# Self-attention: softmax sums taken over two rounds at a time, and causal masks added behind two products

## What is computed

```python
q = (x @ Wq.T + bq).reshape(B, T, H, D)      # H = 16 heads of D = 32
k = (x @ Wk.T + bk).reshape(B, T, H, D)
v = (x @ Wv.T + bv).reshape(B, T, H, D)
scores = jnp.einsum('bqhd,bkhd->bhqk', q, k) * attn_scale[0]
scores = jnp.where(mask[None, None], -jnp.inf, scores)
attn = jax.nn.softmax(scores, axis=-1)
out = jnp.einsum('bhqk,bkhd->bqhd', attn, v).reshape(B, T, C)
return out @ Wo.T + bo
```

## Time and profile before

| | us |
|---|---|
| median of 3 runs | 3718.32 |
| lowest and highest | 3716.07, 3718.48 |
| the profiled execution | 3677.42 |
| its span, first to last instruction | 3675.7 |
| of it self-attention, about | 0 to 1825 |

### The profile page before, as it was taken

How to read it: one execution, slowest core, us unless ns; L and a number is a source line. 1 busy time by engine, 2 the same in 40 slices (tenths; PEclk the granted TensorE clock), 3 DMA queues, 4 the chain that set the end, 5 groups by cost and what they waited for, 6 DMA issues and landing times. The chain is left out here.

```text
span 3675.7 us, 65297 instructions
## 1 busy us (share of the span) xinstructions
PE 3247.4 (88%) x20385; PEld 2065.6 (56%) x20385; DVE 2202.0 (60%) x4409; ACT 1380.6 (38%) x3155; POOL 909.5 (25%) x889
## 2 busy tenths in 40 slices
PE   8998989899899998999797899999698892999991
PEld 4444444454444544444343677776577771888881
DVE  4645546455464544646354688887377773777775
ACT  2443434434343443434421466665000000444441
POOL 2000000000000000000032333333266665566661
PEclk8999999999999999999998999999899996999995
DMA  4122121221212222021075121211222212799996
GB/s 118 39 67 71 38 62 39 70 68 47 60 32 70 68 56 70 13 75 29 25 244 185 50 66 61 68 61 56 94 55 57 60 52 81 222 248 254 251 252 211
DMA packets 186637, 344.01 MB, mean 94 GB/s; under 512 B 36153, under 2 KB 53946, under 8 KB 185402
## 3 DMA queue, kind: packets, MB, share of 16 engines
q1 hardware_dynamic: 127674, 234.12, 22.5%
q0 software_dynamic: 31360, 56.82, 6.4%
q10 hardware_dynamic: 27392, 50.34, 3.7%
HBM read 206.96 MB, written 83.89 MB: 79 GB/s over the span
## 5 line engine op out<-in xcount | busy, mean ns | idle before, releaser
L549 DVE TENSOR_REDUCE sa_pmax<-sa_w 128x1 f32<-128x512 f32 (+3 forms) x1280 | 690.9, 603 | 398.9 <-PE sa_w L358 233.7
L491 ACT ACTIVATE sa_probs<-sa_s 128x512 f32<-128x512 f32 (+3 forms) x1280 | 614.0, 534 | 809.4 <-PE sa_s L393 416.7
L355 PE MATMUL sa_w<-sa_parts 96*128 96x512 f32 (+3 forms) x1280 | 488.2, 440 | 81.5 <-DVE sa_pmax L549 34.0
L393 PE MATMUL sa_s<-sa_parts 128*128 128x512 f32 (+3 forms) x1280 | 463.8, 416 | 23.5 <-ACT sa_probs L491 22.1
L296 POOL DMA_DIRECT2D scratch_attention_T<-sa_oT x32 | 17.6, 550 | 1782.7 <-DVE sa_oT L592 1519.7
L355 PEld LDWEIGHTS sa_w<-sa_parts 96*128 96x128 f32 x1280 | 236.1, 194 | 331.0 <-issue 178.7
L393 PEld LDWEIGHTS sa_s<-sa_parts 128*128 128x128 f32 x1280 | 241.0, 196 | 141.8 <-ACT sa_probs L491 90.7
L412 PE MATMUL sa_pv<-sa_probs,sa_values 128*32 128x512 f32 (+3 forms) x2560 | 299.8, 540 | 4.6 <-PE sa_w L338 2.4
L416 PE MATMUL sa_pv<-sa_probs,sa_ones 128*32 128x512 f32 (+3 forms) x2560 | 292.9, 528 | 0.0
L1318 POOL DMA_INDIRECT token_and_weight_of_slot<-rt_entry,rt_sl x256 | 256.3, 1001 | 143.1 <-issue 75.2
L1144 ACT ACTIVATE xa_sm<-xa_sm,xa_nmax 128x154 f32<-128x154 f32 x512 | 208.7, 409 | 64.5 <-DVE xa_nmax L1088 64.5
(11 more groups left out here) (242 smaller groups left out, 5704.8 us busy)
## 6 DMA issues: line engine op xcount, KB each, us to landing
ex_w<-in_w SPq DMA_DIRECT2D x138, 512.0 KB, 4.6
sa_parts<-sa_halves SPq DMA_DIRECT2D x384, 128.0 KB, 2.4
sa_xt<-in_xT SPq DMA_DIRECT2D x32, 1024.0 KB
scratch_attention_T<-sa_oT POOLq DMA_DIRECT2D x32, 256.0 KB, 2.5
on_at<-scratch_attention_T SPq DMA_DIRECT2D x32, 256.0 KB, 3.3
on_xr<-in_x SPq DMA_DIRECT2D x32, 256.0 KB, 3.5
scratch_x<-on_xn ACTq DMA_DIRECT2D x32, 256.0 KB, 2.2
scratch_x_T<-on_xnT ACTq DMA_DIRECT2D x32, 256.0 KB, 3.5
```

The source lines that it names most:

```text
L355: mm = nc.tensor.matmul(ps[:, 0:w], qparts[0:3 * HD, h, q0:q0 + P], kparts[0:3 * HD, h, k0:k0 + w], start=True, stop=s != 0)
L393: mm = nc.tensor.matmul(ps[:, 0:w], kparts[:, h, kb * P:(kb + 1) * P], qparts[:, h, q0:q0 + w], start=True, stop=not diag)
L491: nc.scalar.activation(probs[:, r % NPB, h, 0:w], sbank[n % NSB][:, 0:w], ACT.Exp).then_inc(exp_done, 1)
L549: dve.tensor_reduce(pmax[:, j * GH + h, s:s + 1], wbank[b][:, 0:width_], AX.X, ALU.max).then_inc(work_free[b], 1)
```

## The change

1. **Sums over pairs.** GpSimd adds the `probs` of rounds 2p and 2p + 1 into a new tile `both`, and TensorE multiplies `ones` by `both` once for a pair. `both` is one buffer: GpSimd waits for the sums' products of the pair before (`ones_done`) and for the exponentials; TensorE waits for `both_ready`. On the diagonal the first round of a pair is wider by 128 queries; these are copied first, then the rest is added. `probs` gets four buffers.
2. **`weighted` by pairs.** Both rounds' products with `values` and then the sums' products stand behind the next pair's second round. The loop is turned: a pair is peeled in front, and an iteration ends with the next group's pair 0, behind which the last pair's `weighted`, `take_raw`, `take_den` and the last `normalize` now stand.
3. **Masks.** The maxima's segments are ordered by key segment first and head second, and two that both need the mask are issued as product, product, mask, mask; so are the scores of heads 0 and 1. Groups of maxima in a round are cut at 4 and 6 in place of 3 and 5.
4. **Stores.** SyncE issues them in place of GpSimd: stores 0 and 1 behind `spread_parts(it + 1, 0)` and `(it + 1, 1)`, stores 2 and 3 at the end of its iteration, in front of `spread_parts(it + 1, 2)`. Two projections of chunk 3 move by one round.

```diff
     def segments(c):
-        return [(j, h, s) for j in range(QB) for h in range(GH) for s in range(c + 1)]
+        return [(j, h, s) for j in range(QB) for s in range(c + 1) for h in range(GH)]
...
-                 (3, 0): [("k", 0)], (3, 1): [("q", 0)], (3, 5): [("v", 0), ("k", 1)], (3, 6): [("q", 1)], (3, 9): [("v", 1)],
+                 (3, 0): [("k", 0)], (3, 1): [("q", 0)], (3, 5): [("k", 1)], (3, 6): [("v", 0), ("q", 1)], (3, 10): [("v", 1)],
...
-    NPB = 2
+    NPB = 4
...
+            def add_pair(it, p):
+
+                even, odd = 2 * p % NPB, (2 * p + 1) % NPB
+                c, k = round_at[2 * p]
+                wide, w = width(c, kbs(c)[k]), width(c, kbs(c)[k + 1])
+                pool.wait_ge(ones_done, it * NPAIR + (p + 1))
+                pool.wait_ge(exp_done, it * NU + (NSB + 2 * GH * (p + 1)))
+                apart(pool, passed)
+                if wide > w:
+                    pool.tensor_copy(both[:, :, w:wide], probs[:, even, :, w:wide]).then_inc(rest_copied, 1)
+                    pool.wait_ge(rest_copied, it * NREST + (rest_pairs.index(p) + 1))
+                    apart(pool, passed)
+                pool.tensor_tensor(both[:, :, 0:w], probs[:, even, :, 0:w], probs[:, odd, :, 0:w], ALU.add).then_inc(both_ready, 1)
...
+            def weighted(it, p):
+
+                for r in (2 * p, 2 * p + 1):
...
                     for h in range(GH):
                         a = HD * h
-                        nc.tensor.matmul(pvbank[0][a:a + HD, 0:w], values[:, kb, h, :], probs[:, r % NPB, h, 0:w],
-                                         start=first, stop=last)
-                    for h in range(GH):
-                        a = HD * h
-                        mm = nc.tensor.matmul(pvbank[1][a:a + HD, 0:w], ones[:], probs[:, r % NPB, h, 0:w],
-                                              start=first, stop=last)
+                        mm = nc.tensor.matmul(pvbank[0][a:a + HD, 0:w], values[:, kb, h, :], probs[:, r % NPB, h, 0:w],
+                                              start=kb == NKB - 1, stop=kb == QB * chunk_q(c))
                     mm.then_inc(pv_done, 1)
...
+                pe.wait_ge(both_ready, it * NPAIR + (2 + p + 1))
+                for h in range(GH):
+                    a = HD * h
+                    mm = nc.tensor.matmul(pvbank[1][a:a + HD, 0:w], ones[:], both[:, h, 0:w],
+                                          start=k == 1, stop=kb == QB * chunk_q(c))
+                mm.then_inc(ones_done, 1)
...
+                    maxima(it, i, segs[:4])
+                    score_masks([scores(it, r, 0), scores(it, r, 1)])
+                    maxima(it, i, segs[4:6])
+                    score_masks([scores(it, r, 2)])
+                    maxima(it, i, segs[6:])
+                    score_masks([scores(it, r, 3)])
```

More of the change, by code:

```diff
@@ L127, in free_at @@
         return it * uses[b] + (pre_uses[b] + WORK[key] // NWB + 1)
+    rest_pairs = [p for p in range(NR // 2) if rounds(round_at[2 * p][0]) - round_at[2 * p][1] <= QB]
+    NREST = len(rest_pairs)
     NSB = 3
-    NPB = 2
+    NPB = 4
+    NPAIR = NR // 2
     NDIST = 3 * GH * 16
@@ L188, in each_group, with each_from_second @@
             body(ITERS - 1, False)
+        def each_from_second(eng, pair):
+            with eng.Fori(0, ITERS - 1) as it:
+                for p in range(1, NPAIR):
+                    pair(it, p, True, (it, p - 1))
+                pair(it + 1, 0, True, (it, NPAIR - 1))
+            for p in range(1, NPAIR):
+                pair(ITERS - 1, p, False, (ITERS - 1, p - 1))
         @block.sync
@@ L372, in _ @@
             pe.wait_ge(consts_set, 1)
[L373 to L374 removed]
+            maxima(None, 0, [("m", 0, n) for n in range(len(segments(0)))])
             shift(None, 0, 0)
[L376 to L399 removed]
@@ new lines, in _, with scores @@
+            maxima(None, 0, [("m", 1, n) for n in range(EARLY)])
+            def scores(it, r, h):
+                c, k = round_at[r]
+                kb = kbs(c)[k]
+                n = GH * r + h
+                w = width(c, kb)
+                q0 = chunk_q(c) * CH
+                if k == 0:
+                    pe.wait_ge(shift_ready, it * (NC * GH) + (GH * c + h + 1))
+                pe.wait_ge(exp_done, it * NU + (n + 1 if n else NSB))
+                ps = sbank[n % NSB]
+                diag = kb < QB * (chunk_q(c) + 1)
+                mm = nc.tensor.matmul(ps[:, 0:w], kparts[:, h, kb * P:(kb + 1) * P], qparts[:, h, q0:q0 + w],
+                                      start=True, stop=not diag)
+                if not diag:
+                    mm.then_inc(s_ready, 1)
+                    return None
+                return ps[:, w - P:w]
@@ L400, in weighted, with score_masks @@
+            def score_masks(blocks):
+                for ps in blocks:
+                    if ps is not None:
+                        nc.tensor.matmul(ps, identb[:], maskT[:], start=False, stop=True).then_inc(s_ready, 1)
+            def weighted(it, p):
+                for r in (2 * p, 2 * p + 1):
                     c, k = round_at[r]
@@ L425, in body, with pair @@
+            def pair(it, p, more, behind):
+                for r in (2 * p, 2 * p + 1):
+                    c, k = round_at[r]
                     on_next = c == NC - 1
+                    i = it + 1 if on_next else it
                     segs = maxima_in(c, k) if more or not on_next else []
-                    maxima(segs[:3])
-                    scores(r, 0)
-                    scores(r, 1)
-                    maxima(segs[3:5])
-                    scores(r, 2)
-                    maxima(segs[5:])
@@ L441, in body @@
                             keys_queries(it, i, key[0], key[1])
-                    if r >= 1:
-                        weighted(r - 1)
-                weighted(NR - 1)
-            each_group(pe, body)
+                if behind is not None:
+                    weighted(*behind)
+            pair(0, 0, True, None)
+            each_from_second(pe, pair)
+            weighted(ITERS - 1, NPAIR - 1)
         @block.scalar
```

192 lines of the change are left out of this document (91 added, 101 removed).

## The result

The changed kernel takes 3772.41 us (median of four), the kernel before 3717.2 us: a ratio of 1.016, with a 95% interval of 1.015 to 1.018. One of the four executions was disturbed (4642 us): it is left out of the ratio but counted in that median, which would be 3769.68 us without it. The forecast was 3596 us, with a range of 3545 to 3655 us; the time lies 117 us above its end, and the sign is wrong. The profiled execution took 3766.8 us, its span 3764.9 us, 89 us more than the span of before.

The account below looks back on a forecast made before the run. TensorE was taken as the limit in places, VectorE's three banks nearly as close, ScalarE limiting rounds without maxima. Sums 114 + masks 12 - jump 3.5 = 122 us, off 3718.3 us, gave 3596 us; range 3545 to 3655 us.

Parts of the forecast that it names:

- What bounds the kernel: Self-attention: TensorE is the limit in places, ScalarE or VectorE's banks in others; TensorE is busy 94% of the loop.
- three kinds of rounds: Self-attention: rounds without maxima (3.47 us), rounds with maxima (4.64 us), and the jump back at a group's end.
- the part on the jump: Group's end: four maxima ahead of the scores lose 0.5 us at each of seven jumps, 3.5 us; bounds 0 and 10.
- chunk 2's pairs: Chunk 2's full pairs with maxima: 8.6 us against 9.28 us; 0.6 us gain taken for each of four.
- Masks, 12 us, bounds 0 and 48: 344 neighbouring pairs of masks on TensorE: each pair issued together saves 0.05 us, 0.7 of it counted; 12 us.
- The row that I read against a covered weight load: Earlier trace: a mask's weight load starts only at 240.03, so such loads aren't already covered and grouping gains.
- The sums, 114 us: All groups of self-attention: sums' products once for a pair save 14.7 us a group, 11.3 us in the last.
- a chunk's last pair: Narrow pairs of chunks 0 to 2: 0.3 us gain each, since `shift` waits for the last maxima anyway.
- GpSimd's adding costs nothing: Pairs' adds on GpSimd: 4.2 us each, needed by TensorE after 5.44 us at the tightest, so no cost.
- The slower rival: GpSimd's add slowed by other engines' memory use, TensorE waiting: no change at 8.3 us, 3768 us at 9; chance 0.08.
- The slow clock stays: Seven jumps: the same two idle times and the same 10 us of slow clock at each.
- Jump and SyncE's queue: Group's end: the jump loses 3.5 us; spreading chunk 2's parts behind store 3 costs nothing, with 2 us margin.

Follow-up runs that it names:

- the pairs alone: The changed kernel with the old order of segments, old cuts and each mask right behind its product: ratio 0.986 to the kernel before.
- the trace with the scores' masks: The changed kernel with old order, cuts and maxima's masks, keeping sums over pairs and the scores' masks two at a time: ratio 0.985 to the kernel before.
- the version with cuts at 2 and 4: Sums over pairs, scores' masks grouped, values' products each round, multiply on GpSimd, maxima cut at 2 and 4: 3543.7 us, ratio 0.964 to the kernel before.

## Why the prediction was wrong, point by point

- **What bounds the kernel**: held. Of the three kinds of rounds that I named, the rounds with maxima decide; I said there that VectorE's banks are as near to the limit as TensorE, and then didn't ask what the diff does to exactly those banks.
- **The failed step: the cuts.** The text knows them only as "four maxima now stand ahead of the scores", in the part on the jump, priced at 7 x 0.5 = 3.5 us with bounds of 0 and 10 us. They stand in every round with four maxima or more, not in seven jumps. Measured: 2.3% of the time on the kernel before, 2.5% in the changed kernel and 1.6% on the pairs alone, 60 to 93 us where I had 3.5 us. The prediction had all that was needed: "three products can be ahead of VectorE" stands in its own working of chunk 2's pairs, and the earlier trace rows has the 0.54 us and 0.59 us. 0.54 + 0.59 us less the 0.92 us of three products is a wait of 0.2 us at least, in each of the rounds, with two scores behind it. The pair length of 8.6 us was worked out with the old cuts; the pair of rounds 4 and 5 of chunk 2 measured 8.6 us with them and 9.6 us with the new ones. The larger part is in chunk 3, 77.7 us with the old cuts and 85.7 us with the new ones in the changed kernel.
- **Masks, 12 us, bounds 0 and 48**: wrong in sign under the new cuts, and the bounds didn't reach below nothing. With the old cuts neither grouping is told apart from nothing; with the new ones both together lose 1.1%, most likely since a grouped product is handed over later. Holding back a finished result was a cost that I didn't look for. The row that I read against a covered weight load is weak as well: the load at 240.03 lies inside the product recorded from 239.77 to 240.19.
- **The order of `segments`**: not priced. 0.2 to 0.3%, not clear of its interval.
- **The sums, 114 us**: the mechanism was right, the size was double. The pairs alone give 1.4%, 52 us of 3706. The term fails in places. Pairs without maxima take 6.29 us for a forecast of 6.41. Chunk 2's pairs at rounds 2, 4 and 8 take 9.5, 8.6 and 8.9 us, for 9.9, 9.4 and 9.9 us before and 8.6 us forecast. But a chunk's last pair, for which I said only that `shift` waits for the last maxima anyway, grew, and so did the pair with the scaling: TensorE waits for `mcol` and for VectorE behind GpSimd (rounds 6 and 7 of chunk 2, with the scaling: 12.2 us for 9.7 us). By the starts of the scores in the traces, chunk 1 takes 52.1 us a group for 50.6 before, where I had 3.0 us less (49.2 us in the trace with the scores' masks), and chunk 2 53.9 for 53.0, where I had 3.1 less; chunks 3 and 0 together are 9.1 us shorter, for 8.5 us forecast.
- **GpSimd's adding costs nothing**: its own time was right (4.57 us for 2048 columns, inside 3.61 to 5.10; 1.8 us of wait for it in all). The timeline of TensorE and GpSimd in the changed kernel's rounds without maxima answers to the earlier trace rows:

```profile
914.62 0.96 PE L428 MATMUL sa_s<-sa_parts 128*128 128x512 f32 x3
915.81 2.46 PE L428 MATMUL sa_s<-sa_parts 128*128 128x512 f32 x5 [0.22 <-ACT sa_probs L539]
918.20 1.92 PE L452 MATMUL sa_pv<-sa_probs,sa_values 128*32 128x512 f32 x16
919.94 1.04 PE L461 MATMUL sa_pv<-sa_both,sa_ones 128*32 128x512 f32 x8
920.91 0.96 PE L428 MATMUL sa_s<-sa_parts 128*128 128x512 f32 x3
...
914.98 4.57 POOL L329 TENSOR_TENSOR sa_both<-sa_probs 128x2048 f32<-128x2048 f32 x1 [9.55 <-PE sa_pv L461]
```

  From 914.62 to 920.91 is 6.29 us, one pair. What was wrong is the side on which I looked for a price: I asked only whether other engines slow the add, and put at nothing what the add does to VectorE. It holds VectorE's multiply, scaling and rounding for the rest of the add; 0.7 to 1.0%, 26 to 36 us.
- **The slower rival** named GpSimd's adding, and the wrong mechanism: it wanted an add of 8.3 us. No add is longer than 4.6 us. That the time came near its 3768 us is chance.
- **The slow clock stays**: wrong. It stays at the jumps, but there are more windows. In the changed kernel, around the jump (columns as in the earlier trace rows):

```profile
762.00:765.70 3.70, 2.10 (x13) 1.24 (x11) 2.53 (x5) 0.96 (x2) 0.00 (x0) 1.00 0.00 0
765.70:769.10 3.40, 3.40 (x9) 1.71 (x8) 0.69 (x1) 1.58 (x4) 0.00 (x0) 0.50 0.00 0
769.10:775.90 6.80, 3.92 (x31) 1.65 (x30) 3.33 (x3) 1.27 (x2) 2.59 (x2) 1.00 0.02 5
775.90:786.20 10.30, 5.00 (x23) 4.03 (x23) 4.97 (x12) 1.42 (x4) 1.45 (x1) 0.50 0.59 138
```

  The last is the jump's; the second, of 3.40 us, follows a stretch in which TensorE was busy 2.10 of 3.70 us. By the granted clock in the trace, self-attention had 9 stretches at 0.50 with 113 us in all, at its start, behind its seven jumps and at its end; now it has 43 with 239 us, 34 of them of 3.4 us. That is 126 us more at half clock, at most 63 us of work lost. In the pairs alone there are 29 (177 us), in the version with cuts at 2 and 4 there are 9 (89 us), fewer us than before the change.
- **Jump and SyncE's queue**: no wait of TensorE for the spreading of parts appears in the waits, as I said. The jump's own cost can't be told apart from the cuts there: with the new cuts alone on the kernel before, the stretch from the start of chunk 3's last pair to the end of chunk 0's first is 3.4 us longer (35.4 against 32.0), where I had 0.5 us.

In sum, step by step from the kernel before to the changed one: pairs -1.4% (forecast -3.1%), order and masks +0.5% (forecast -0.3%), cuts +2.5% (forecast +0.1%), together +1.6%. In another sequence the steps have other sizes: on the kernel before, masks on top of the cuts cost 1.1%. Of the 1.7% that the pairs fall short, undoing the clumped value products gives back 1.0% and making the adds small 0.7 to 1.0%, each by itself; no run has both.

**What stays open.** How much of the loss is the clock. The value block behind a wait for VectorE can take 3.35 us in place of 1.92. But the short stretches at half clock don't simply follow the waits: the kernel before with the new cuts has 12 of them with 80.8 us of waiting for maxima, the changed kernel with the old cuts 24 with 36.0 us. No run changes the one and not the other. The window of the pairs alone in which that block begins:

```profile
822.20:825.80 3.60, 3.60 (x17) 1.10 (x20) 1.80 (x4) 1.19 (x2) 0.00 (x0) 0.60 0.00 0
```

TensorE is busy all of it, at 0.60 of its clock; 1.29 us of waiting for VectorE end 0.9 us ahead of it. Open as well: whether the order alone costs anything, what the turned loop, SyncE's stores and the moved projections do within the pairs, and by which way the cuts at 2 and 4 gain.

## What to carry to other kernels

Count how many results an engine is asked to issue ahead of other work, and compare it with the number of banks: if the fourth product has three banks, it and everything queued behind it wait for the reader, in every round. Even within the banks, work that others don't wait for is better behind the work that they do: two ahead of the scores beat three here. Price each number that a diff changes in every place where the code runs it, not only in the one where it drew attention. Work moved to an idle engine is not free for the neighbour with which it shares memory: look on the path for short VectorE instructions that grow when a long GpSimd instruction runs beside them, and put them where none runs, or on GpSimd's own queue. And when an experiment leaves out a part of the arithmetic, check that later stages still do the same work.

## What the hardware showed that I had not expected

- A VectorE instruction of 16 columns lasted until a running GpSimd add was over (0.92 us beside a 3.45 us add, and 1279 ns in the mean, for 175 ns without one), while reductions of TensorE's banks, the reciprocal and a small reduction in the on-chip memory kept their times.
- Short idle times of TensorE in an otherwise busy loop, the longest single one 0.3 to 1.5 us, stood ahead of stretches of 3.4 us at 1.2 GHz, 34 of them in the changed kernel, where self-attention before has none.
- The routing of the experts, the same code in all kernels, took 471 to 472 us on two chips and 496 to 521 us on three others.
